# Turning quantized weight codes inside the state-space loop instead of on their later loads

## The reference

```python
x = x + mamba_mixer(layernorm(x), ...)          # W_in, conv, Wx, selective scan over 16 states, W_out
x = x + matmul(fq(layernorm(x)), fq(context))   # 8-bit fake quantization with given scales
# feed-forward; fake_quant: per row s = max|t| / 127, q = round(t / s) * s
gate = fake_quant(h) @ fake_quant(w_gate).T     # w_gate, w_up: 2752 x 1024
up   = fake_quant(h) @ fake_quant(w_up).T
x = x + fake_quant(silu(gate) * up) @ fake_quant(w_down).T
```

## Time and profile before

| | us |
|---|---|
| median of 3 runs | 1680.31 |
| lowest and highest | 1670.72 and 1685.57 |
| the profiled execution | 1669.6 |
| its span | 1667.8 |

### The profile page before, as it was taken

How to read it: one execution, slowest core, us unless ns; L and a number is a source line. 1 busy time by engine, 2 the same in 40 slices (tenths; PEclk the granted TensorE clock), 3 DMA queues, 4 the chain that set the end, 5 groups by cost and what they waited for, 6 DMA issues and landing times. The chain is left out here.

```text
span 1667.8 us, 17950 instructions
## 1 busy us (share of the span) xinstructions
PE 1408.3 (84%) x5576; PEld 727.8 (44%) x5576; DVE 1335.1 (80%) x1641; ACT 929.3 (56%) x1375; POOL 946.3 (57%) x767
## 2 busy tenths in 40 slices
PE   6999577788888987768898888888999994999898
PEld 3444344444444443444454454444434442444443
DVE  6585899999999979999999988889047556777684
ACT  1211557768768655867767767755234122556670
POOL 0000679889899878879999898897100000333300
PEclk9999788999999999877999999999999996999899
DMA  7597333443453432433683682664473103589504
GB/s 275 201 351 261 92 118 107 169 145 107 152 162 108 169 101 96 140 100 111 216 274 113 225 273 82 237 217 158 168 290 132 54 26 94 137 189 192 121 3 174
DMA packets 155468, 264.38 MB, mean 159 GB/s; under 512 B 76560, under 2 KB 94096, under 8 KB 149552
## 3 DMA queue, kind: packets, MB, share of 16 engines
q1 hardware_dynamic: 151056, 236.27, 43.9%
q10 hardware_dynamic: 4320, 27.00, 4.4%
HBM read 207.60 MB, written 38.60 MB: 148 GB/s over the span
## 5 line engine op out<-in xcount | busy, mean ns | idle before, releaser
L1093 DVE TENSOR_TENSOR_SCAN hbuf<-decay,hbuf 128x512 f32<-128x512 f32 x492 | 587.2, 1208 | 24.0 <-ACT decay L788 23.5
L788 ACT ACTIVATE decay<-delta,chan_sb 128x512 f32<-128x512 f32 x492 | 334.2, 686 | 281.9 <-DVE hbuf L1093 280.4
L598 PE MATMUL turn<-ident,hbuf 128*128 128x128 f32 x2048 | 338.2, 295 | 179.2 <-DVE hbuf L1093 128.7
L598 PEld LDWEIGHTS turn<-ident,hbuf 128*128 128x128 f32 x2048 | 255.1, 150 | 450.6 <-DVE hbuf L1093 199.6
L1107 DVE SCALAR_TENSOR_TENSOR acc<-turn,pn,acc 128x512 f32<-128x512 f32 x360 | 262.2, 728 | 41.1 <-PE turn L598 40.1
L927 POOL TENSOR_TENSOR hbuf<-wout,sx 128x512 f32<-128x512 f32 x172 | 216.0, 1289 | 15.0 <-DVE wout L1080 15.0
L927 POOL TENSOR_TENSOR hbuf<-du,sx 128x512 f32<-128x512 f32 x172 | 218.5, 1305 | 1.7 <-DMA sx<-bt_scratch 1.7
L948 POOL TENSOR_TENSOR acc<-acc,part 128x512 f32<-128x512 f32 x120 | 153.1, 1276 | 52.1 <-ACT part L798 51.0
L1796 PE MATMUL bank<-codes,wout 128*128 128x512 bf16 (+1 forms) x704 | 153.9, 382 | 1.0 <-PEq L1210 1.0
L580 PE MATMUL bank_g<-wout,codes 128*128 128x512 f32 x256 | 136.9, 622 | 0.0
L510 PE MATMUL bank_u<-wout 128*128 128x512 f32 x224 | 113.2, 625 | 3.7 <-DMA wout<-in_wu 2.8
(11 more groups left out here) (217 smaller groups left out, 2171.0 us busy)
## 6 DMA issues: line engine op xcount, KB each, us to landing
wout<-in_woutT SPq DMA_DIRECT2D x48, 512.0 KB, 4.2
sx<-bt_scratch SPq DMA_DIRECT2D x86, 256.0 KB, 3.7
codes<-in_wg SPq DMA_DIRECT2D x8, 2048.0 KB, 9.3
ubuf<-u_scratch SPq DMA_DIRECT2D x16, 1024.0 KB, 6.6
wout<-in_w_gate SPq DMA_DIRECT2D x26, 512.0 KB, 4.8
wout<-in_w_up SPq DMA_DIRECT2D x26, 512.0 KB, 4.6
raw_d<-in_w_down ACTq DMA_DIRECT2D x8, 1376.0 KB, 7.0
b_more<-bt_scratch SPq DMA_DIRECT2D x42, 256.0 KB, 3.5
```

The source lines that it names most:

```text
L598: last = pe.transpose(turn[t % 2][:, j * P:j * P + P], hbuf[:, s % 4, j, t * P:t * P + P], ident[:, :])
L788: act.activation(decay_place(q), delta[:, G % 2, j, :], ACT.Exp, scale=a_col(GD * (G % GROUPS) + j, n)).then_inc(dA_done, 1)
L1093: dve.tensor_tensor_scan(h, decay_place(q), h, 0.0, ALU.mult, ALU.add).then_inc(scan_done, 1)
```

## The change

The codes are turned before they are stored, and the later stages load them without a transpose.

- `qcode` shrinks to half a unit (128 x 512) and a tile `qturn` (128 x 4 x 128) of the same size is new. The order of ACT's four operations in a unit becomes scale left, plain left, scale right, plain right, in the same 176 places. With h = 2 u or 2 u + 1 the half, the plain operation of half h waits until half h - 1 has been turned out of `qcode` (`q_turned`).
- SP, for each of 88 halves: stores half h - 1 from `qturn`, waits for ACT's plain operation of half h, waits until the store of h - 1 has landed, and issues a DMA transpose `qcode` to `qturn`. Before it was one store for each of 44 units.
- `wq_dram` is laid out as (block, partition, gate or up, 8, 128). The six loads in `attend` and 38 in `feed_forward` are plain DMAs.
- The semaphore `ms_done` goes; POOL waits for the same point through counts of `norm_step`.

```diff
-        qcode = sb("qcode", [P, H], BF16)
+        qcode = sb("qcode", [P, H // 2], BF16)
+        qturn = sb("qturn", [P, KC // 2, P], BF16)
...
-        RELU_STEP = 9
+        MS_STEP = (7, 21)
+        RELU_STEP = 10
...
-            def store_quant(u):
+            def turn_quant(h):
+                n = unit_rows(h // 2)
+                sp.wait_ge(q_step, 2 * (h + 1))
+                if h >= 1:
+                    sp.wait_ge(q_stored, 16 * h)
+                sp.dma_start(qturn[:, :, 0:n], qcode[0:n, :], transpose=True).then_inc(q_turned, 16)
+
+            def store_quant(h):
+                u, lo = h // 2, KC // 2 * (h % 2)
                 m, c, n = u % 2, u // 2, unit_rows(u)
-                sp.wait_ge(q_step, 4 * (u + 1))
-                sp.dma_start(wq_dram[m, c * P:c * P + n, :], qcode[0:n, :]).then_inc(q_stored, 16)
+                sp.wait_ge(q_turned, 16 * (h + 1))
+                sp.dma_start(wq_dram[c, :, m, lo:lo + KC // 2, 0:n], qturn[:, :, 0:n]).then_inc(q_stored, 16)
...
                         for o in (quant_at(q) if q >= 0 else ()):
+                            if o % 2 == 1:
+                                if o >= 3:
+                                    store_quant(o // 2 - 1)
+                                turn_quant(o // 2)
                             if o % 4 == 3:
-                                store_quant(o // 4)
                                 if o // 4 + 2 < UNITS:
                                     load_quant(o // 4 + 2)
...
                     if G == NG - 1 and n == 10:
+                        store_quant(2 * UNITS - 1)
                         sp.wait_ge(q_step, 4 * UNITS)
...
-                    u, half, plain = o // 4, o % 2, o % 4 >= 2
+                    u, half, plain = o // 4, o % 4 // 2, o % 2 == 1
...
                     if plain:
-                        act.wait_ge(q_step, o - 1)
-                        if u >= 1:
-                            act.wait_ge(q_stored, 16 * u)
-                        act.activation(qcode[0:n, half * 512:half * 512 + 512], v, ACT.Identity, bias=rnd[0:n, 1:2])\
-                            .then_inc(q_step, 1)
+                        act.wait_ge(q_step, o)
+                        if o >= 3:
+                            act.wait_ge(q_turned, 16 * (o // 2))
+                        act.activation(qcode[0:n, :], v, ACT.Identity, bias=rnd[0:n, 1:2]).then_inc(q_step, 1)
...
             def rms(b):
-                pool.wait_ge(ms_done, b + 1)
+                pool.wait_ge(norm_step, MS_STEP[b])
...
-                    sp.dma_start(keep.wT[:, c, m, :, :], wq_dram[m, c * P:c * P + P, :], transpose=True).then_inc(wT_in, 16)
+                    sp.dma_start(keep.wT[:, c, m, :, :], wq_dram[c, :, m, :, :]).then_inc(wT_in, 16)
...
-                    sp.dma_start(wT[:, c % WT, m, :, 0:r], wq_dram[m, c * P:c * P + r, :], transpose=True)\
+                    sp.dma_start(wT[:, c % WT, m, :, 0:r], wq_dram[c, :, m, :, 0:r])\
                         .then_inc(wT_load[c % WT], 16)
...
-    wq_dram = nc.dram_tensor("wq_scratch", (2, INTER, H), BF16, kind="Internal").ap()
+    wq_dram = nc.dram_tensor("wq_scratch", (OC, P, 2, KC, P), BF16, kind="Internal").ap()
```

More of the change, by code:

```diff
@@ L167, in mixer @@
         norm_step = sem("norm_step")
-        ms_done = sem("ms_done")
         rs_done = sem("rs_done")
@@ L196, in mixer @@
         q_step = sem("q_step")
+        q_turned = sem("q_turned")
         q_stored = sem("q_stored")
@@ L476, in _ @@
             sp.wait_ge(yT_loaded, 16 * (TT + 2))
-            sp.wait_ge(q_stored, 16 * UNITS)
+            sp.wait_ge(q_stored, 32 * UNITS)
         @block.tensor
@@ L1055, in mean_squares @@
                 link(dve.tensor_scalar(rs[:, :, 0:1], rs[:, :, 0:1], 1.0 / R, RMS_EPS, ALU.mult, ALU.add))
+                nc_[0] += 1
                 dve.tensor_scalar(rs[:, :, 1:3], rs[:, :, 1:3], 1.0 / N, RMS_EPS, ALU.mult, ALU.add)\
-                    .then_inc(ms_done, 1)
+                    .then_inc(norm_step, 1)
             def normalise(b):
```

## The result

| kernel | median us | ratio to the kernel before, 95% interval |
|---|---|---|
| before | 1675.51 (4 runs) | |
| changed | 1726.18 (1718.59 to 1729.45, 4 runs) | 1.0298 (1.0257 to 1.034) |
| changed, measured again | 1725.56 (6 runs) | 1.0279 (1.0254 to 1.0305) |

Forecast was 1680 with a range of 1668 to 1700. The kernel is about 50 us slower, outside the range. The span of the profiled execution went from 1667.8 to 1716.8 us. The last row stands beside its own runs of the kernel before (median 1676.75).

A forecast was written before the change was run, and what follows sets the result against it. It took DVE to bound the scan and PE gate and up; 1669.6 (profiled execution) + 0 (ACT) + 1.5 (weight rows) - 1.5 (drain) = 1669.6, forecast as a median of 1680, range 1668 to 1700.

The forecast's parts named there:

- Bounds of the kernel: Whole kernel: DVE sets the scan's pace, 93% then 90% busy; PE bounds gate and up.
- ACT waits for the turn: Loop, ACT before its plain operations: no wait at a 3.0 us landing, term 0, with 28 us as other end.
- The later stages: Attend and gate/up, loads without transpose: nothing in attend, 1.5 us off (0 to 3) in the drain of gate/up.
- Issue of a turn: Loop, SP's queue: issuing a 4-tile transpose takes 0.65 us, at 0.16 us per tile.
- The ceiling I had named: Loop, SP's queue: upper limit for issuing a 4-tile turn, the whole 1.31 us of 8 tiles from DRAM.
- What is queued behind SP: Loop, loads behind SP's new waits: weight rows of the output projection come late, adding 1.5 us (0 to 6).
- 29 us of summed lateness: Output projection's 48 row loads: late by 29 us in sum at the slower values, a fifth of them waited for.
- 12.9 us in 11 waits: Output projection before the change: PE's waits for weight rows in the two-slot ring, 12.9 us.
- three signs that I had named: Forecast wrong if turns land above 4.5 us median, a turn's issue exceeds 1.3 us, or gate products take under 150 us.
- PE waits for the output projection's rows: Rival, output projection: slower by 6 us with both directions at the ceiling, 1686, chance 0.08.
- ACT waits: Rival, loop: one `qcode` and one `qturn` make ACT wait for turns, 10 to 28 us, about 1698, chance 0.17.

The follow-up runs named there:

- e10: The changed kernel with a plain copy in place of each turn and two plain 512-byte DMAs issued ahead of each copy: 1738.81 us, ratio 1.0361.
- e6: The changed kernel with the output projection's two rows issued ahead of store and turn in SP's order: 1747.04 us, ratio 1.0435.
- e2: The changed kernel with each turn replaced by a plain DMA of the same bytes, all waits kept: 1712.86 us, ratio 1.0208.
- e7: The changed kernel with two turned tiles and no operations on codes in the 24 steps that load the output projection's rows: 1673.42 us, ratio 0.999.

## Why the prediction was wrong, point by point

**Bounds of the kernel.** Right for the first 800 us and for gate and up. In groups 5 to 7 I named DVE, at 90% busy, and did not ask what its other 10% were: of 37.6 us in which it idled there, 24.4 ended with a state turned by PE. PE's waits for rows already stood in the earlier trace rows.

**ACT waits for the turn.** Right in the main: 6.9 us in 6 waits, and the scan's own wait for decays grew by 1.6 us only. The turn lands in 2.5 us in the median, where I took 3.0.

**The later stages.** Right: from the first gate product to the spread of the peak 158.4 us (1463.41 to 1621.85) against 160.2 (1413.11 to 1573.27), 1.7 us less where I took 1.5.

**Issue of a turn.** Mis-sized: 0.65 us by tiles, 1.20 measured. It isn't in proportion to the tiles: from SBUF four cost 1.20 us and 22 cost 3.31, and four from SBUF nearly what eight from DRAM did. The ceiling I had named, 1.31, was nearer. It may be worth 12 to 15 us, by the account under e10.

**What is queued behind SP.** This is the step that failed: 1.5 us (0 to 6) for the rows of the output projection. Measured, groups 5 to 7 are 46.0 us longer, and PE's wait for rows is 45.7 us instead of 7.2. Three things went wrong in it.
1. *The store's landing.* I took 2.5 us, the median over the loop. In groups 5 to 7 of the very same trace it is 3.6 us, and there the new order puts it right behind two rows of 512 KB and a row of B: 4.4 us in the median, up to 9.5. For these landings alone SP stands 131.4 us in 30 waits there, 4.4 us each; from the start of a store's issue to the turn it is 5.2 us, in 29 cases. The landings before and changed, and the stand:

```profile
DMA to landing us min/median/max: 2.1/3.6/6.0
```
```profile
DMA to landing us min/median/max: 3.0/4.4/9.5
```
```profile
SPq L332 <- DMA wq_scratch<-qturn: 131.4, 30, 8.0
```
2. *The slack of the rows.* A slot is filled once in a step of 7.2 us; the load lands in 4.2 us in the median and the products of a row take about 2 us, which leaves some 1 us (an estimate from these three). A stand of 4.4 us and 1.2 us of issue in three steps of four don't fit. I looked for rows that would come late against their old issue times and did not do this subtraction.
3. *The feedback.* I laid turns and stores between SP's issue rows of before, each at its old time at the earliest, so a late row delayed only itself. But a row's issue waits for PE, PE for the row before, and the step for PE. In this ring a delay isn't absorbed by the next wait; it is that wait. My 29 us of summed lateness were of the right order as a sum, against 46; a fifth of them was not. That the sum is near may be chance, as it was laid out with landings that were too short.

A reading error came with it: 12.9 us in 11 waits counts the weight load (7.2 us in 6) and the product (5.7 in 5) of mostly the same waits. The proper comparison is 7.2 with 45.7. The three signs that I had named as showing the forecast wrong (landing of a turn, its issue, the gate products) all stayed on the side of the forecast; none of them looked at the stand for the store.

**The rivals.** "PE waits for the output projection's rows" was the right mechanism, with a chance of 0.08 and a price of 6 us, where 46 was due. "ACT waits" had the right sign but isn't what happens in the changed kernel. e6, 72 us slower than the kernel before with 88.8 us of such waits, shows that it was one reordering away.

## What to carry to other kernels

A wait for a DMA to land, put on a queue that issues other engines' loads, costs what the tightest load behind it can't absorb: for each transfer behind the wait, subtract landing time and use from the time between two fills of its slot, and compare with the stand, with landing times from that stretch and not from the whole loop. If a wait sits in a ring (load, product, slot free, load), what exceeds the slack comes again at each fill: here 131 us of stands made the three groups 46 us longer, far from the 1.5 us of the forecast and also from the full price. The cure was a second buffer behind the transfer and keeping the waits out of the steps that feed the ring; putting the rows first, with one tile on each side, only moved the wait to ACT, at a higher price.

## What the runs showed of the hardware

Issuing a DMA transpose of four 128 x 128 tiles from SBUF took SP 1.20 us, eight from DRAM 1.31 us and 22 from SBUF 3.31 us at best, against 0.47 us for a plain copy of the same 128 KB as the four tiles. The Trainium skill says transposing DMAs are as fast as regular ones ("Advanced Engine Details and Errata", X-Bar Transpose). For the transfer that holds here to within 0.5 us: the turn of 128 KB landed in 2.5 us in the median, the copy of e2 in 2.0, and e7 made 88 turns at no measurable cost. For the issuing queue it doesn't hold, by 0.73 us each.
